# Counting GpSimd's row gathers on three semaphores in turn, in an attention and codebook-FFN kernel

## The chip, the core and the metric

The kernel runs on one core of one Trainium2 chip. The metric is the device time of one execution in microseconds (us). The profile's span, from the first to the last instruction, is a little shorter than that time.

## What is computed

The input is x, 2048 tokens by 512 features, in float32. Four small layers of width 64 run first (layer norm, a long convolution by a decaying complex exponential, a two-matrix feed-forward), then a residual and a layer norm. Behind them stands a feed-forward block whose three weight matrices are stored as rows of a codebook:

```python
CS, CB, H, I = 8, 8192, 512, 1376        # codebook: 8192 rows of 8 float32
Wg = codebook[idx_gate].reshape(I, H)    # idx_gate, idx_up: (1376, 64)
Wu = codebook[idx_up].reshape(I, H)
Wd = codebook[idx_down].reshape(H, I)    # idx_down: (512, 172)
g = einsum('bsh,ih->bsi', x, Wg)
u = einsum('bsh,ih->bsi', x, Wu)
y = einsum('bsi,hi->bsh', silu(g) * u, Wd)
x = layernorm(x + y)
```

## The kernel before

Everything stays in the core's on-chip memory, and each engine has its program written out by hand, in order. Semaphores tie the engines together; there is no scheduler. The 1376 inner rows are cut into 11 tiles (`TILES`), ten of 128 rows and the last, `FULL`, of 96.

**Gate and up** weights are made by TensorE: VectorE compares indices that SyncE has spread over the partitions (`bc`) with a column of numbers to get `one_hot` (line 839), TensorE multiplies it with the codebook into `cand` (`candidates`, line 538), VectorE picks the right row with `chosen` (line 857), and TensorE sums it up (`add_up`, line 550). Such a step of four columns is a quad; there are 352. A first part of the quads runs between the pieces of the small layers, in the slots of the loop at line 681 (`SLOTS`, 22 of them); the rest between the products of the feed-forward tiles (`hidden`, `down`, loop at line 788).

**Down** weights are made by GpSimd. For tile k it issues 64 indirect DMAs (4 blocks `q` of 16 columns `j`; 48 for the last tile), each of which gathers 128 codebook rows of 32 bytes, one per partition, into `stage_down[k % RING]`. `RING` is 3, so three tiles of down weights can stand ready. There are 688 gathers in all, and after its first few constants GpSimd does nothing else. Each gather adds 16 to its semaphore when it has landed. Two waits hold GpSimd in this loop (lines 285 to 296):

- `turned_down`: before tile k from 3 on, until TensorE has transposed tile k - 3 and so freed its buffer;
- `down_in`: at every fourth gather (`BURST`), until all gathers begun so far have landed.

TensorE's `turn_down(k, n)` (line 737) waits for its bank and for `down_in`, then transposes the four blocks of the tile (line 748) into `bank[2]`. ScalarE (`down_hi`) and VectorE (`down_lo`) copy them out as `wd`. `turn_down` stands once in each tile of the loop, after slot 4 or 3 (`TURN_DOWN`), long before `down` uses `wd`.

Of the kernel before, what the change touches and what calls it, by code (L numbers as in the profile page):

```python
# [25 lines left out]
def build(nc, a, out):  # L26
# [3 lines left out]
    CB, CS = a["L0_ffn_codebook"].shape  # L30
# [5 lines left out]
    KT = V // P  # L36
# [5 lines left out]
    JD = P // CS  # L42
# [13 lines left out]
    BCS = 4  # L56
    RING = 3
    SUB = 32
    BURST = 4
    EARLY = 8  # L60
    PER_SLOT = 2
    SLOTS = ITEMS + 6
# [28 lines left out]
    with ctx:  # L91
# [3 lines left out]
        def sem(name):  # L95
            return ctx.enter_context(nc.semaphore(name))
# [22 lines left out]
        with setup_ctx, attn_ctx:  # L119
# [3 lines left out]
            def at(name, shape, dt=F32):  # L123
                return sb(name, shape, dt, attn_ctx)
# [26 lines left out]
            turn = at("turn", [P, L, P])  # L151
# [21 lines left out]
        for c in range(NC):  # L173
# [12 lines left out]
            sq2_made var2 rs2_made normed2 spread ff_made ff_back h_made hn_made  # L186
            attn_out x_added stats_made aggregated rstd_made shift_made x1_made x1_turned x1_hi x1_lo
            bc_in0 bc_in1 bc_in2 bc_in3 one_hot_made candidates chosen_made summed picked_hi picked_lo
            down_in turned_down w_hi w_lo gate_made up_made gate_silu product act_hi_made act_lo_made
            down_made down_added out_normed stored""".split()  # L190
        s = {n: sem(n) for n in sem_names}

# [66 lines left out]
        @block.gpsimd  # L259
        def _(pool):  # L260
            pool.memset(ident[:, :], 0.0).then_inc(s["consts_made"], 1)
            pool.memset(perm[:, :], 0.0).then_inc(s["consts_made"], 1)
            pool.wait_ge(s["consts_made"], 2)
            pool.affine_select(out=ident[:, :], in_=ident[:, :], compare_op=ALU.not_equal, fill=1.0, base=0,
                               pattern=[[-1, P]], channel_multiplier=1).then_inc(s["masks_made"], 1)
            pool.affine_select(out=perm[:, :], in_=perm[:, :], compare_op=ALU.not_equal, fill=1.0, base=-D,
                               pattern=[[-1, P]], channel_multiplier=1).then_inc(s["masks_made"], 1)
            pool.wait_ge(s["masks_made"], 2)
            pool.affine_select(out=perm[:, :], in_=perm[:, :], compare_op=ALU.not_equal, fill=1.0, base=D,
                               pattern=[[-1, P]], channel_multiplier=1).then_inc(s["masks_made"], 1)  # L270
            pool.memset(adder[:, :], 0.0).then_inc(s["consts_made"], 1)
            pool.wait_ge(s["consts_made"], 3)
            block8 = adder[:, SUB - CS:SUB]
            pool.memset(block8, 1.0).then_inc(s["consts_made"], 1)
            pool.iota(iota_low[:, :], pattern=[[P, LT]], base=0, channel_multiplier=1).then_inc(s["iotas_made"], 1)
            pool.iota(iota_m[:, :], pattern=[[0, 1]], base=0, channel_multiplier=1).then_inc(s["iotas_made"], 1)
            pool.wait_ge(s["consts_made"], 4)
            pool.affine_select(out=block8, in_=block8, compare_op=ALU.is_ge, fill=0.0, base=0,
                               pattern=[[-HIGH, CS]], channel_multiplier=1).then_inc(s["masks_made"], 1)
            pool.wait_ge(s["masks_made"], 4)  # L280
            pool.affine_select(out=block8, in_=block8, compare_op=ALU.is_ge, fill=0.0, base=HIGH - 1,
                               pattern=[[HIGH, CS]], channel_multiplier=-1).then_inc(s["masks_made"], 1)
            pool.wait_ge(s["index_down_in"], 16)
            begun = 0
            for k in range(TILES):
                if k >= RING:
                    pool.wait_ge(s["turned_down"], k - RING + 1)
                for q in range(KT):
                    for j in range(JD if k < FULL else REST // CS):
                        if begun and begun % BURST == 0:  # L290
                            pool.wait_ge(s["down_in"], 16 * begun)
                        column = k * JD + j
                        pool.indirect_dma_start(stage_down[k % RING][:, q, j * CS:(j + 1) * CS], None, a["L0_ffn_codebook"],  # L293
                                                bass.IndirectOffsetOnAxis(ap=idx_down[:, q, column:column + 1], axis=0)
                                                ).then_inc(s["down_in"], 16)
                        begun += 1

        @block.scalar
# [211 lines left out]
        def _(pe):  # L510
# [226 lines left out]
            def turn_down(k, n):  # L737


                if k % 2:  # L740
                    pe.wait_ge(s["w_lo"], k)
                elif k:
                    pe.wait_ge(s["down_added"], NT * (k // 2))
                else:
                    pe.wait_ge(s["x1_lo"], NT)
                pe.wait_ge(s["down_in"], 16 * KT * (k * JD + n // CS))
                for q in range(KT):
                    done = pe.transpose(bank[2][0:n, q * P:(q + 1) * P], stage_down[k % RING][:, q, 0:n], ident[:, :])  # L748
                done.then_inc(s["turned_down"], 1)
# [38 lines left out]
            for k in range(FULL):  # L788
                shares = SHARES[k % 2]
                quads = quads_of(k)  # L790
                for slot in range(len(quads) + 1):
                    if slot < len(quads):
                        candidates(quads[slot])
                        add_up(quads[slot] - 1)
                    if 1 <= slot <= NC * shares:
                        c, share = divmod(slot - 1, shares)
                        hidden(k, P, c, share, shares)
                    if slot == TURN_DOWN[k % 2]:
                        turn_down(k, P)
                    if k % 2 and 0 <= slot - FIRST_DOWN < NT:  # L800
                        down(k, P, (0, 1), slot - FIRST_DOWN, (bank[2][:, :],))
            add_up(ALL_QUADS - 1)
            for c in range(NC + 1):
                if c < NC:
                    hidden(FULL, REST, c, 0, 1)
                if c == 0:
                    turn_down(FULL, REST)
                else:
                    for t in range((c - 1) * TPC, c * TPC):
                        down(FULL, REST, (0,), t, (bank[2][:, :], cand[0][:, :], cand[1][:, :], cand[2][:, :]))  # L810
# [374 lines left out]
```

## Time and profile before

| | us |
|---|---|
| median of three runs | 1478.64 (1478.60 to 1478.94) |
| the profiled execution | 1478.19 |
| its span | 1476.4 |
| TensorE busy in it | 1404.5 (95%) |
| VectorE busy | 1131.9 (77%) |
| GpSimd busy | 718.8 (49%) |
| ScalarE busy | 272.2 (18%) |

The rows further down come from this one profiled execution. "idle before, releaser" is the time an engine stood still before an instruction and what ended it. In a timeline row "x4" means four instructions of one kind, merged; overlapping matmuls make a merged row longer than its distance to the next. "issue" is time in which the engine waited for nothing that the profile shows. The granted TensorE clock is given as a share of full speed.

### The profile page before, as it was taken

How to read it: one execution, taken by the hardware profiler on the slowest of the kernel's cores; microseconds unless marked ns; L12 is line 12 of the kernel's file. 1: busy time of each engine (PE TensorE's matmuls, PEld its weight loads, DVE VectorE, ACT ScalarE, POOL GpSimd, SP SyncE). 2: the span in 40 equal slices, each digit the busy share in tenths (PEclk: the TensorE clock that was granted, in tenths of full speed). 3: DMA queues.
4: the chain of work that ended last, by engine and by line, in shares of the span. 5: the costliest groups of instructions: out<-in, count | busy, mean ns of one | idle time of the engine just before them, and what ended most of it. 6: DMA issues, size and time to landing. Idle time of an engine off the chain costs nothing.

```text
span 1476.4 us, 21752 instructions
## 1 busy us (share of the span) xinstructions
PE 1404.5 (95%) x7795; PEld 951.5 (64%) x7795; DVE 1131.9 (77%) x2508; ACT 272.2 (18%) x458; POOL 718.8 (49%) x703
## 2 busy tenths in 40 slices
PE   6869999977999999999999999999999999999995
PEld 4535555444666776666776666776666776678873
DVE  4998888766777768787768787778877778887656
ACT  3336666523100000000000000000000000001005
POOL 4656655552265655555555656655555555500000
PEclk9989999877999999999999999999999999999997
DMA  8222212111233323333223333223333223322103
GB/s 209 39 64 47 53 46 52 39 32 23 80 85 85 75 54 81 85 85 86 75 54 82 82 88 82 67 64 82 85 84 80 67 66 83 86 74 66 46 20 114
DMA packets 94065, 105.68 MB, mean 72 GB/s; under 512 B 43966, under 2 KB 48838, under 8 KB 93959
## 3 DMA queue, kind: packets, MB, share of 16 engines
q1 hardware_dynamic: 67908, 96.45, 22.0%
q0 software_dynamic: 22016, 2.86, 5.5%
q10 hardware_dynamic: 4034, 4.98, 1.1%
q8 instruction: 63, 1.03, 0.3%
q14 instruction: 44, 0.35, 0.1%
HBM read 99.32 MB, written 4.90 MB: 71 GB/s over the span
## 4 chain that ended last, share of the span: by engine, by line
PE 91%; DVE 4%; issue 2%; ACT 1%; SPq 1%; DMA 1%; ACTq 0%; DVEq 0%
PE bank L512 46%; PE cand L512 44%; DVE one_hot L839 1%; DMA book_in<-in_L_ffn_codebook 1%; PE bank L668 1%; DVE work L823 0%; SPq L226 0%; DVE stats L1007 0%; DVE x1t_lo L823 0%; ACT x L394 0%; ACT xt L328 0%; DVE chosen L857 0%; PE bank L748 0%; DVE x L823 0%; ACT x1t_hi L398 0%
## 5 line engine op out<-in xcount | busy, mean ns | idle before, releaser
L293 POOL DMA_INDIRECT stage_down<-in_L_ffn_codebook,idx_down x688 | 716.7, 1042 | 573.0 <-DMA stage_down<-in_L_ffn_codebook,idx_down 347.9
L512 PE MATMUL cand<-one_hot,book 128*128 128x512 f32 (+1 forms) x2816 | 729.8, 402 | 12.3 <-DVE one_hot L839 12.1
L512 PEld LDWEIGHTS cand<-one_hot,book 128*128 128x128 f32 x2816 | 532.5, 192 | 151.7 <-issue 19.2
L839 DVE TENSOR_SCALAR one_hot<-bc,low_of 128x512 fp32r<-128x512 uint16 (+1 forms) x1408 | 584.3, 477 | 0.3
L857 DVE SCALAR_TENSOR_TENSOR chosen<-bc,high_of,cand 128x512 f32<-128x512 uint16 (+1 forms) x352 | 258.5, 734 | 222.9 <-PE cand L512 221.5
L512 PE MATMUL bank<-x1t_hi,w 128*128 128x512 f32 (+1 forms) x704 | 254.2, 418 | 0.7 <-DVE w L823 0.7
L512 PEld LDWEIGHTS bank<-x1t_hi,w 128*128 128x128 f32 (+1 forms) x704 | 125.8, 185 | 51.2 <-issue 29.2
L512 PE MATMUL bank<-chosen,adder 128*32 128x128 f32 (+1 forms) x2816 | 148.6, 283 | 3.8 <-DVE chosen L857 3.8
L512 PE MATMUL bank<-x1t_lo,w 128*128 128x512 f32 (+1 forms) x352 | 147.4, 419 | 0.0
L512 PEld LDWEIGHTS bank<-chosen,adder 128*32 128x32 f32 x2816 | 55.5, 108 | 133.9 <-issue 129.4
L512 PE MATMUL bank<-wd,act_hi 128*128 128x512 f32 (+1 forms) x328 | 106.4, 406 | 0.1
L347 ACT ACTIVATE w<-bank 128x128 fp32r<-128x128 f32 (+1 forms) x88 | 24.0, 272 | 440.3 <-PE bank L512 440.3
L823 DVE TENSOR_TENSOR x<-x,bank 128x512 f32<-128x512 f32 x100 | 68.1, 681 | 28.1 <-PE bank L512 27.9
L512 PEld LDWEIGHTS bank<-x1t_lo,w 128*128 128x128 f32 (+1 forms) x352 | 65.2, 185 | 23.8 <-issue 14.3
L466 ACT ACTIVATE prod<-bank 128x512 f32<-128x512 f32 (+1 forms) x44 | 26.3, 598 | 290.4 <-PE bank L512 290.4
L470 ACT ACTIVATE act_hi<-prod 128x512 fp32r<-128x512 f32 (+1 forms) x44 | 27.9, 634 | 271.8 <-DVE prod L823 271.8
L512 PEld LDWEIGHTS bank<-wd,act_hi 128*128 128x128 f32 (+1 forms) x328 | 58.4, 188 | 18.6 <-issue 6.7
L512 PE MATMUL bank<-wd,act_lo 128*128 128x512 f32 (+1 forms) x164 | 64.4, 393 | 0.0
L512 PE MATMUL bank<-work,mean_p 128*128 128x512 f32 x72 | 35.8, 614 | 6.0 <-issue 5.6
L823 DVE TENSOR_TENSOR prod<-prod,bank 128x512 f32<-128x512 f32 (+1 forms) x44 | 29.9, 679 | 10.7 <-PE bank L512 10.6
L512 PEld LDWEIGHTS bank<-wd,act_lo 128*128 128x128 f32 (+1 forms) x164 | 30.8, 188 | 7.2
L512 PE MATMUL bank<-work,w1t 64*128 64x512 f32 x64 | 31.8, 617 | 1.3 <-DVE work L1061 1.2
(163 smaller groups left out, 713.8 us busy)
## 6 DMA issues: line engine op xcount, KB each, us to landing
bc<-index_parts SPq DMA_DIRECT2D x320, 256.0 KB
stage_down<-in_L_ffn_codebook,idx_down POOLq DMA_INDIRECT x688
bc<-index_parts_rest SPq DMA_DIRECT2D x32, 192.0 KB
x<-in_L_attn_x ACTq DMA_DIRECT2D x4, 1024.0 KB, 9.9
out_x<-x SPq DMA_DIRECT2D x16, 256.0 KB, 2.0
index_parts<-parts_t SPq DMA_DIRECT2D x20, 32.0 KB, 1.9
w_in<-in_L_attn_W ACTq DMA_DIRECT2D x2, 256.0 KB, 8.5
idx_down<-in_L_ffn_idx_down SPq DMA_DIRECT2D x1, 344.0 KB, 7.1
```

The source lines that it names most:

```text
L293: pool.indirect_dma_start(stage_down[k % RING][:, q, j * CS:(j + 1) * CS], None, a["L0_ffn_codebook"], bass.IndirectOffsetOnAxis(ap=idx_do ...
L347: act.activation(w[group % WRING][:, 0, 0:nw], bank[3 + group % 2][:, 0:nw], ACT.Copy).then_inc(s["picked_hi"], 1)
L466: act.activation(prod[0:n, c % 2, :], bank[0][0:n, :], ACT.Silu).then_inc(s["gate_silu"], 1)
L470: act.activation(act_hi[0:n, k % 2, c * C:(c + 1) * C], prod[0:n, c % 2, :], ACT.Copy).then_inc(s["act_hi_made"], 1)
L512: return pe.matmul(dst, lhs, rhs, start=start, stop=stop)
L668: done = pe.transpose(bank[2][:, k * P:(k + 1) * P], x[:, tile, k * P:(k + 1) * P], ident[:, :])
L823: return v.tensor_tensor(o, x0, x1, op)
L839: done = v.tensor_scalar(one_hot[quad % 2][:, q, 0:nw], bc[quad % BCS][:, 0:nw], low_of[:, q:q + 1], None, ALU.is_equal)
L857: v.scalar_tensor_tensor(chosen[quad % 2][:, 0:nw], bc[quad % BCS][:, nw:2 * nw], high_of[:, 0:1], cand[quad % 3][:, 0:nw], ALU.is_equal, ...
```

## The change

The single counter `down_in` becomes three, `down_in0` to `down_in2`. The gathers take them in turn: gather number `begun` adds to counter `begun % 3`. Before each gather from the fourth on, GpSimd waits until the earlier gathers of the same counter have landed, which is the gather three places ahead. The drain at every fourth gather is gone. TensorE's `turn_down` waits for all three counters, each up to the number of its gathers in the tiles so far. Buffers, gathers, their order and their tiles stay as they are.

```diff
-    BURST = 4
+    IN_FLIGHT = 3
...
                     for j in range(JD if k < FULL else REST // CS):
-                        if begun and begun % BURST == 0:
-                            pool.wait_ge(s["down_in"], 16 * begun)
+                        turn, before = begun % IN_FLIGHT, begun // IN_FLIGHT
+                        if before:
+                            pool.wait_ge(s[f"down_in{turn}"], 16 * before)
                         column = k * JD + j
                         pool.indirect_dma_start(stage_down[k % RING][:, q, j * CS:(j + 1) * CS], None, a["L0_ffn_codebook"],
                                                 bass.IndirectOffsetOnAxis(ap=idx_down[:, q, column:column + 1], axis=0)
-                                                ).then_inc(s["down_in"], 16)
+                                                ).then_inc(s[f"down_in{turn}"], 16)
                         begun += 1
...
-                pe.wait_ge(s["down_in"], 16 * KT * (k * JD + n // CS))
+                landed = KT * (k * JD + n // CS)
+                for turn in range(IN_FLIGHT):
+                    pe.wait_ge(s[f"down_in{turn}"], 16 * ((landed + IN_FLIGHT - 1 - turn) // IN_FLIGHT))
```

GpSimd's instructions, from the end of tile 2's gathers to the start of tile 3's, were these (the name in brackets is the semaphore waited for):

```order
L293 DMA stage_down2<-in_L0_ffn_codebook,idx_down 128x8 [waits down_in]
L293 DMA stage_down2<-in_L0_ffn_codebook,idx_down 128x8 x3
L293 DMA stage_down0<-in_L0_ffn_codebook,idx_down 128x8 [waits down_in,turned_down]
L293 DMA stage_down0<-in_L0_ffn_codebook,idx_down 128x8 x3
L293 DMA stage_down0<-in_L0_ffn_codebook,idx_down 128x8 [waits down_in]
```

And now:

```order
L294 DMA stage_down2<-in_L0_ffn_codebook,idx_down 128x8 [waits down_in0]
L294 DMA stage_down2<-in_L0_ffn_codebook,idx_down 128x8 [waits down_in1]
L294 DMA stage_down2<-in_L0_ffn_codebook,idx_down 128x8 [waits down_in2]
L294 DMA stage_down0<-in_L0_ffn_codebook,idx_down 128x8 [waits down_in0,turned_down]
L294 DMA stage_down0<-in_L0_ffn_codebook,idx_down 128x8 [waits down_in1]
L294 DMA stage_down0<-in_L0_ffn_codebook,idx_down 128x8 [waits down_in2]
```

No gather has moved; a wait stands before each of them, where it stood before one in four.

On TensorE, the stretch around the first `turn_down` read:

```order
L512 MATMUL bank<-x1t_hi,w 128x512 [waits x_added]
L748 MATMUL bank<-ident,stage_down 128x128 [waits down_in,x1_lo]
L748 MATMUL bank<-ident,stage_down 128x128 x3
L512 MATMUL cand<-one_hot,book 128x512 [waits chosen_made,one_hot_made]
L512 MATMUL cand<-one_hot,book 128x512 x7
```

And now:

```order
L513 MATMUL bank<-x1t_hi,w 128x512 [waits x_added]
L751 MATMUL bank<-ident,stage_down 128x128 [waits down_in1,down_in2,down_in0,x1_lo]
L751 MATMUL bank<-ident,stage_down 128x128 x3
L513 MATMUL cand<-one_hot,book 128x512 [waits chosen_made,one_hot_made]
L513 MATMUL cand<-one_hot,book 128x512 x7
```

The transposes stay in their place and carry two waits more, in each of the 11 tiles.

## Rows read from the trace of the kernel before

**Rows 1.** The page's chain that ended last, shares of the span by engine.

```profile
PE 91%; DVE 4%; issue 2%; ACT 1%; SPq 1%; DMA 1%; ACTq 0%; DVEq 0%
```

**Rows 2.** Busy time (x instructions) of PE, PEld, DVE, ACT, POOL; clock, DMA.

```profile
389.00:1292.00 903.00, 901.50 (x5330) 633.99 (x5330) 701.58 (x1485) 64.34 (x142) 517.17 (x496) 1.00 0.32 78
```

**Rows 3.** GpSimd's waits: total us, times, longest.

```profile
POOL stage_down L293 <- DMA stage_down<-in_L_ffn_codebook,idx_down: 347.9, 169, 4.7
POOL stage_down L293 <- PE bank L748: 41.2, 1, 41.2
```

**Rows 4.** GpSimd's timeline where tile 9 ends: start, us, [idle before <-releaser].

```profile
1201.03 1.16 POOL L293 DMA_INDIRECT stage_down<-in_L_ffn_codebook,idx_down  x1 [0.30 <-issue]
1204.83 1.15 POOL L293 DMA_INDIRECT stage_down<-in_L_ffn_codebook,idx_down  x1 [2.64 <-DMA stage_down<-in_L_ffn_codebook,idx_down]
```

**Rows 5.** Gathers by stretch: PE, PEld, POOL busy (x instructions) on `stage_down`; clock, DMA.

```profile
123.00:200.00 77.00, 0.00 (x0) 0.00 (x0) 46.20 (x44) 1.00 0.22 48
200.00:280.00 80.00, 0.00 (x0) 0.00 (x0) 44.40 (x42) 1.00 0.23 52
280.00:349.00 69.00, 0.00 (x0) 0.00 (x0) 40.94 (x43) 0.73 0.13 26
```

**Rows 6.** TensorE's timeline around the transposes of tile 0, and of tile 9.

```profile
389.04 0.63 PE L512 MATMUL bank<-x1t_hi,w 128*128 128x512 f32 x2
389.51 0.60 PE L748 MATMUL bank<-ident,stage_down 128*128 128x128 f32 x4
389.87 2.11 PE L512 MATMUL cand<-one_hot,book 128*128 128x512 f32 x8
...
1332.37 0.60 PE L748 MATMUL bank<-ident,stage_down 128*128 128x128 f32 x4
```

**Rows 7.** One line's instructions: duration ns min/median/max, first and last start.

```profile
L293 POOL DMA_INDIRECT stage_down<-in_L_ffn_codebook,idx_down x688: 938/947/2333, 9.1 to 1291.9; - x172
L1081 DVE TENSOR_TENSOR_SCAN work<-cols,state,work x12: 1284/1284/1335, 104.1 to 261.8; 128x512 f32<-128x512 f32 x12
```

**Rows 8.** By form, busy us, mean ns: DVE 349 to 389, DVE and POOL 1180 to 1290.

```profile
L839 DVE TENSOR_SCALAR one_hot<-bc,low_of 128x512 fp32r<-128x512 uint16 x32 | 13.3, 480 | 0.0
...
L839 DVE TENSOR_SCALAR one_hot<-bc,low_of 128x512 fp32r<-128x512 uint16 x125 | 53.2, 488 | 0.0
...
L293 POOL DMA_INDIRECT stage_down<-in_L_ffn_codebook,idx_down x59 | 61.5, 1042 | 48.8 <-DMA stage_down<-in_L_ffn_codebook,idx_down 32.0 <-issue 16.9
```

**Rows 9.** TensorE's timeline: the same matmuls at three slots of the small layers.

```profile
146.22 1.98 PE L512 MATMUL bank<-work,w2t 128*128 128x512 f32 x4
...
157.47 1.98 PE L512 MATMUL bank<-work,w2t 128*128 128x512 f32 x4
...
202.27 1.98 PE L512 MATMUL bank<-work,w2t 128*128 128x512 f32 x4
...
213.60 1.98 PE L512 MATMUL bank<-work,w2t 128*128 128x512 f32 x4
```

**Rows 10.** The chain of waits at the start: start, us, what.

```profile
14.10 0.04 issue
14.14 11.62 DMA book_in<-in_L_ffn_codebook
```

**Rows 11.** GpSimd's timeline from its first gather.

```profile
9.06 1.11 POOL L293 DMA_INDIRECT stage_down<-in_L_ffn_codebook,idx_down  x1 [5.89 <-DMA idx_down<-in_L_ffn_idx_down]
...
18.62 0.94 POOL L293 DMA_INDIRECT stage_down<-in_L_ffn_codebook,idx_down  x1 [4.71 <-DMA stage_down<-in_L_ffn_codebook,idx_down]
...
26.18 1.11 POOL L293 DMA_INDIRECT stage_down<-in_L_ffn_codebook,idx_down  x1 [2.88 <-DMA stage_down<-in_L_ffn_codebook,idx_down]
```

**Rows 12.** TensorE's timeline, three output projections of the small layers.

```profile
285.16 6.87 PE L512 MATMUL bank<-woutt,work 65*128 65x512 f32 x8 [1.20 <-ACT work L441]
...
309.22 7.10 PE L512 MATMUL bank<-woutt,work 65*128 65x512 f32 x8
...
329.54 7.10 PE L512 MATMUL bank<-woutt,work 65*128 65x512 f32 x8
```

**Rows 13.** The page's DMA queue of the gathers: packets, MB, share of 16 engines.

```profile
q0 software_dynamic: 22016, 2.86, 5.5%
```

More of the change, by code:

```diff
@@ L188, in build @@
             bc_in0 bc_in1 bc_in2 bc_in3 one_hot_made candidates chosen_made summed picked_hi picked_lo
-            down_in turned_down w_hi w_lo gate_made up_made gate_silu product act_hi_made act_lo_made
+            down_in0 down_in1 down_in2 turned_down w_hi w_lo gate_made up_made gate_silu product act_hi_made act_lo_made
             down_made down_added out_normed stored""".split()
```

## The prediction

> **What bounds the kernel now.** I read four views, in this order. First the chain that ended last: TensorE holds 91% of it, and neither GpSimd nor a gather appears in it [rows 1]. Then the busy time of the long stretch in which the feed-forward tiles run, 389 to 1292 us: TensorE is busy for 901.50 of 903.00 us at the full clock, while GpSimd issues its last 496 gathers [rows 2]. So from 389 us on the time is TensorE's own instructions. Then GpSimd's waits: it stands 347.9 us for gathers to land, 169 times, and once, for 41.2 us, for TensorE to free a buffer [rows 3]. The reader is to see that these are large numbers on an engine that nobody waits for. The last view says how far nobody waits: the last gather of tile 9 starts at 1201.03 and has landed before the next starts at 1204.83 [rows 4]; TensorE transposes that tile at 1332.37 [rows 6], 127.5 us later. I worked the same distance out for the other ten tiles and it is larger in each (134 us for the last, 153 or more for the rest). The down weights are early everywhere.
>
> **What the change does to GpSimd.** A drain costs, from the start of the fourth gather to the start of the next, 3.80 us at the end of tile 9 [rows 4]; over the whole trace half of the drains lie between 2.6 and 3.4 us. Without a wait a gather follows the one ahead after its own time plus 0.30 us: 0.95 + 0.30 = 1.25 at the least [rows 4, 7], and 1.04 + 0.30, some 1.35 to 1.40, as a mean [rows 4, 8]. A burst of four now takes about 3 x 1.38 + 2.95 = 7.1 us, or 1.77 per gather. In the changed kernel the gather three places ahead began 3 x 1.38 = 4.1 us before. Its landing is due 2.6 to 3.4 us after its start, up to 4 in a tenth of the cases, so the new wait is nearly always over when it is reached. What a finished wait costs on GpSimd no row shows; the chain's smallest piece between two instructions of a queue is 0.04 us [rows 10], and I take 1.38 + 0.05 = 1.43 us per gather. Below, it can't be under 1.25; above, if a finished wait were as dear as the 0.30 us step, 1.7.
>
> At 1.43 us, tiles 0 to 2 (192 gathers) are issued by 9.06 + 275 = 284 us instead of 349, and then GpSimd waits for TensorE's transposes of tile 0 at 389.51 [rows 6], 105 us instead of 41. From there each tile takes 64 x 1.43 = 92 us where TensorE uses a tile in about 107, so GpSimd stands at nearly every tile for `turned_down`, 10 to 30 us each time. The last gather starts near 1192 instead of 1292. The 347.9 us for landing shrink to under 40, and most of it comes back as waiting for TensorE. The change swaps one wait off the path for another off the path. The gain on the end is **0**.
>
> **What it puts on the path.** Four terms, none of them seen in the trace as such.
>
> (a) TensorE has two waits more at each of 11 transposes, 22 in all. Queued behind them is all that TensorE does, so their price would count in full. Today the first transpose carries two waits. The two matmuls ahead start at 389.04, the transposes at 389.51, 0.235 us per matmul, the same pace as without a wait [rows 6]; so two finished waits are hidden under a matmul of 512 columns. All counters are 127 us and more past their value. Lower end 0. Upper end: two more are not hidden at all and cost 0.07 each (a little over the 0.04 of [rows 10]): 22 x 0.07 = 1.5 us. I take 0, the nearest row.
>
> (b) At the start the chain runs through the load of the codebook, `book_in`, 14.14 to 25.76 [rows 10]. Gathers run beside it: two bursts, eight gathers, begin before it lands [rows 11]. A gather takes 0.055 x 1476 / 688 = 0.12 us of all 16 DMA engines [rows 13, 7]. In turn, with the slow landings of this stretch, there would be between 6 (three per 9.56 us, the time from the first gather to the end of the first drain) and 13 (one per 1.3 us). That is -2 to +5 gathers, -0.2 to +0.6 us. I take 0: the landings here are slow, which holds the rate near today's.
>
> (c) From 123 to 280 us, in the slots of the small layers, TensorE and VectorE hand work to and fro, and a delay of VectorE can reach the end. Today 44 + 42 = 86 gathers start there [rows 5]; at 1.43 us it would be 157 / 1.43 = 110, or 24 more. What does a gather do to VectorE? With GpSimd silent (349 to 389) a `one_hot` compare takes 480 ns, with 59 gathers beside it (1180 to 1290) 488 ns [rows 8]. That is 125 x 8 ns = 1.0 us for 59 gathers, 0.017 us each. Upper end 24 x 0.017 = 0.4 us. Lower end 0: two whole slots of TensorE are 157.47 - 146.22 = 11.25 us with 7 gathers started in them, and 213.60 - 202.27 = 11.33 with 5 [rows 9], so more gathers didn't make a slot longer. I take 0.
>
> (d) From 280 to 349 us all but about three of 43 gathers leave [rows 5]. By the same 0.017 us that gives back up to 0.7 us, and by the slots 0. I take 0.
>
> A rule of the Trainium skill speaks against (c). The trace shows that gathers and VectorE do meet, and who loses: a gather lasts 947 ns as a median and up to 2333, while VectorE's longest instruction of the slots, the scan, lasts 1284 and at most 1335 [rows 7]. The Trainium skill, page "SBUF — State Buffer", section "Who interferes with whom", says that the two engines share a pair of ports under an exclusive lock, that the loser is blocked for a whole instruction, and that it is issue order that decides who loses. By that rule a denser stream of gathers would win more often. The trace agrees only for the gathers' side, and the sum above stays with the rows.
>
> **The sum.** 0 + 0 + 0 + 0 + 0, against the profiled execution's 1478.19 us (span 1476.4 and 1.8 outside it). That execution lies 0.45 under the median of the runs, so I forecast on the median: **1478.6 us**. The ends of the terms give -0.2 - 0.7 = -0.9 and 1.5 + 0.6 + 0.4 = +2.5; with 0.3 for the spread of the runs the forecast's own range is 1477.4 to 1481.4.
>
> **The rivals.**
>
> *Gathers hold VectorE (slower).* Place: the slots, 123 to 280 us. Price: if each of the 24 added gathers stopped VectorE for its whole 0.94 us on the path, 22.6 us: 1501. It decides from the point at which VectorE's instructions there lengthen, or start late, by over 0.13 us per added gather (3 us over 24). For it: VectorE is busy for 64 of 73 us in these slots, with little room. Against: the scan grew by 51 ns at most [rows 7], and slots don't follow the number of gathers [rows 9]. Also, no gather is added in total before 389 us, so what is lost in the slots is in part returned by 349. Chance 0.03.
>
> *Waits on TensorE are dear (slower).* If the two added waits at each transpose cost as much as the whole 0.235 us that now hides two, each, it is 22 x 0.235 = 5.2 us: 1483.8. Against: the pace before the transposes is untouched by the two that are there [rows 6]. Chance 0.02.
>
> *The granted clock of 280 to 389 us moves (either way).* TensorE stands idle often enough there for its clock to fall: the mean was 0.73 of full over 280 to 349 [rows 5], so between its levels of 1.2 and 2.4 GHz it was at the lower half the time. From one projection to the next it took 309.22 - 285.16 = 24.06 us and then 20.32 [rows 12]. The work is nearly the same; 3.7 us is what such a stretch can win or lose by where the low clock falls. With the gathers gone from here VectorE could hand over earlier or the pattern could shift: 1474.9 (chance 0.04) or 1482.3 (0.03). Against: three executions agree within 0.34 us, so the pattern is stable.
>
> *The change does not do what it says.* If landings are slower one behind the other, or each wait costs as much as a drain's share, gathers stay at 1.77 us and GpSimd ends near 1290. The time is the same, 1478.6. Chance 0.02.
>
> **How the numbers follow.** The forecast has 0.86. It and the last rival lie within 0.2% (3.0 us, about what a measurement of this kernel can tell from no change): 0.88 same. Faster is the clock's one side, 0.04. Slower is 0.03 + 0.02 + 0.03 = 0.08. The forecast's own range leaves out all rivals but the last, 0.12 in all, and takes in the ends of every unknown cost, so it is the range given.
>
> **What would show it right or wrong.** In the profile of the changed kernel: GpSimd's waits for landing fall from 347.9 us to under 40 and its waits for TensorE rise from 41 us to some 250; gathers in a row start 1.43 us apart (1.25 to 1.7); tiles 0 to 2 are issued by about 284 us, the last gather starts near 1192. TensorE's transposes are at 389.5 and 1332.4 within 1 us, with no gap ahead of them (term a). `book_in` lands at 25.8 within 0.6 (b). The slots of the small layers stay at 11.25 us, `one_hot` at 480 ns (c). If a transpose ever waits for a gather, or if the compares or the scan grow by a tenth, my reading of what is off the path is wrong.

## The result and the profile after

| | time, us | against before on the same chip |
|---|---|---|
| before | 1478.62 (1477.45 to 1478.94) | |
| changed | 2205.18 (2190.93 to 2207.99) | 1.489 [1.486, 1.493] |

The changed kernel is 49% slower where I had forecast no change. The page of the profiled execution, 2207.99 us with a span of 2206.2, has TensorE at 67% of the span. The chain that ended last was nearly TensorE alone in [rows 1] (91%); now TensorE holds 57%, a quarter has no known releaser, and an eighth is "issue", time in which an engine waited for nothing that the profile shows:

```profile
PE 1488.9 (67%) x7795; PEld 986.0 (45%) x7795; DVE 1127.9 (51%) x2508; ACT 272.1 (12%) x458; POOL 669.3 (30%) x703
...
PE 57%; another core or an unknown queue 24%; issue 12%; DVE 5%; ACT 1%; DMA 0%; SPq 0%; DVEq 0%; ACTq 0%
...
L294 POOL DMA_INDIRECT stage_down<-in_L_ffn_codebook,idx_down x688 | 667.2, 970 | 1200.1 <-PE bank L751 974.9
```

The waits of all engines in the changed kernel (us in total, times, longest) read on from there:

```profile
POOL stage_down L294 <- PE bank L751: 974.9, 8, 332.9
DVE chosen L860 <- remote: 684.2, 31, 55.7
ACT prod L467 <- remote: 485.5, 8, 77.3
...
PE bank L513 <- DVE chosen L860: 258.3, 24, 32.4
...
PE bank L513 <- issue: 172.8, 25, 31.5
...
POOL stage_down L294 <- DMA stage_down<-in_L_ffn_codebook,idx_down: 11.4, 11, 2.9
```

GpSimd did what the change says: its waits for landings went from the 347.9 us of [rows 3] to 11.4, and gathers follow each other at 0.95 + 0.30 = 1.25 us. At the end of each stream it waits for TensorE. The news is in the others. VectorE starts `chosen` up to 55.7 us late, on data that the profile can't place ("remote", though there is one core).

Where the time goes is seen by stretches of the changed kernel: the stream of tiles 0 to 2, the pause until the first transposes, the stream of tile 3, and what follows. The columns are those of [rows 2]:

```profile
9.10:261.50 252.40, 66.14 (x283) 41.42 (x281) 49.55 (x206) 22.30 (x40) 186.54 (x192) 0.60 0.18 30
261.50:593.40 331.90, 278.27 (x1167) 153.16 (x1168) 251.78 (x509) 154.21 (x222) 0.00 (x0) 0.88 0.15 43
594.20:676.50 82.30, 30.40 (x144) 18.43 (x142) 17.15 (x37) 1.24 (x3) 62.13 (x64) 0.65 0.15 26
676.50:780.00 103.50, 82.85 (x480) 56.57 (x480) 62.12 (x134) 7.09 (x15) 23.16 (x24) 0.90 0.23 63
```

The first of these stretches in the kernel before:

```profile
9.10:261.50 252.40, 228.20 (x1018) 128.46 (x1017) 213.00 (x526) 131.34 (x186) 147.05 (x140) 0.95 0.30 67
```

While gathers run without a pause, everything else crawls: of 252 us TensorE is busy for 66, where it was busy for 228, and ScalarE for 22 in place of 131. Once they stop, the others work again. TensorE's transposes of the down weights date the delay, changed kernel first:

```profile
L751 PE MATMUL bank<-ident,stage_down x44: 270/272/274, 593.4 to 2160.7; 128*128 128x128 f32 x40, 128*96 128x128 f32 x4
```

```profile
L748 PE MATMUL bank<-ident,stage_down x44: 270/272/273, 389.5 to 1430.9; 128*128 128x128 f32 x40, 128*96 128x128 f32 x4
```

The first ones start at 593.4 in place of 389.5 us, 204 us late; the last ones are 730 us late. So 526 us came in the eight single tiles that were streamed after the first three, 66 us for each.

How an engine is held shows in the changed kernel's timeline in the stream of tile 3 (start us, us, what, [idle before <-releaser]); the matmuls shown are five of the eight of one `cand` group, which has neither wait nor signal between its matmuls:

```profile
641.03 0.59 PE L513 MATMUL cand<-one_hot,book 128*128 128x512 f32 x1 [0.74 <-issue]
641.71 0.95 POOL L294 DMA_INDIRECT stage_down<-in_L_ffn_codebook,idx_down  x1 [0.30 <-issue]
...
642.96 0.95 POOL L294 DMA_INDIRECT stage_down<-in_L_ffn_codebook,idx_down  x1 [0.30 <-issue]
643.12 0.59 PE L513 MATMUL cand<-one_hot,book 128*128 128x512 f32 x1 [1.50 <-issue]
...
648.02 0.59 PE L513 MATMUL cand<-one_hot,book 128*128 128x512 f32 x1 [2.21 <-issue]
...
650.82 0.59 PE L513 MATMUL cand<-one_hot,book 128*128 128x512 f32 x1 [2.21 <-issue]
...
653.62 0.59 PE L513 MATMUL cand<-one_hot,book 128*128 128x512 f32 x1 [2.21 <-issue]
```

Each matmul takes its 0.59 us. They start 2.09 and later 2.80 us apart, where they need no more than their own time. An instruction that waits for nothing is held too, so it is not a late semaphore alone. And the work itself did not grow: VectorE is busy for 1127.9 us in all, where it was busy for 1131.9, and ScalarE for 272.1 in place of 272.2. GpSimd's own steps stay at 0.30 us.

### The profile page after: what moved, and what is told of

It reads as the page before. It is cut to its first block, busy times and chain, and to the rows that moved or that the text cites. A ratio compares the mean times of both kernels' runs of the same rounds, so it can differ in the third digit from the quotient of the medians.

```text
span 2206.2 us, 21763 instructions
## 1 busy us (share of the span) xinstructions
PE 1488.9 (67%) x7795; PEld 986.0 (45%) x7795; DVE 1127.9 (51%) x2508; ACT 272.1 (12%) x458; POOL 669.3 (30%) x703
## 2 busy tenths in 40 slices
DMA packets 94064, 105.68 MB, mean 48 GB/s; under 512 B 43965, under 2 KB 48837, under 8 KB 93958
## 4 chain that ended last, share of the span: by engine, by line
PE 57%; another core or an unknown queue 24%; issue 12%; DVE 5%; ACT 1%; DMA 0%; SPq 0%; DVEq 0%; ACTq 0%
PE bank L513 29%; PE cand L513 28%; DVE one_hot L842 2%; DVE chosen L860 0%; DVE stats L1010 0%; PE bank L669 0%; DVE x L826 0%; DMA work<-in_L_ffn_idx_gate 0%; DVE act_lo L826 0%; DVE prod L826 0%; DVE x1t_lo L826 0%; ACT x L395 0%; PE bank L751 0%; ACT xt L329 0%
## 5 line engine op out<-in xcount | busy, mean ns | idle before, releaser
L294 POOL DMA_INDIRECT stage_down<-in_L_ffn_codebook,idx_down x688 | 667.2, 970 | 1200.1 <-PE bank L751 974.9
L513 PE MATMUL cand<-one_hot,book 128*128 128x512 f32 (+1 forms) x2816 | 777.6, 415 | 138.4 <-issue 120.3
L513 PEld LDWEIGHTS cand<-one_hot,book 128*128 128x128 f32 x2816 | 552.7, 199 | 302.3 <-issue 164.7
L513 PE MATMUL bank<-chosen,adder 128*32 128x128 f32 (+1 forms) x2816 | 154.6, 293 | 386.5 <-DVE chosen L860 258.3
L513 PE MATMUL bank<-x1t_hi,w 128*128 128x512 f32 (+1 forms) x704 | 270.0, 441 | 12.1 <-issue 11.4
L513 PEld LDWEIGHTS bank<-x1t_hi,w 128*128 128x128 f32 (+1 forms) x704 | 133.9, 197 | 67.4 <-issue 44.3
L513 PE MATMUL bank<-x1t_lo,w 128*128 128x512 f32 (+1 forms) x352 | 155.0, 440 | 7.4 <-issue 7.4
L523 PE MATMUL bank<-ident,idx_low 128*128 128x128 f32 x11 | 4.8, 441 | 107.3 <-issue 99.0
```

What stands on the lines that cost most here:

```text
L513: return pe.matmul(dst, lhs, rhs, start=start, stop=stop)
L523: done = pe.transpose(dst[0:JP, m * P:(m + 1) * P], part[:, k, :], ident[:, :])
```

## The experiments

The kernels ran in five groups ("calls" in the recorded expectations), each group on one chip, no two on the same, with the kernel before beside the others (medians 1476.98 to 1477.75 us in all groups). It turned out to matter which group a kernel ran in, so they are told in their order.

### First group: what is it in the change?

Three edits of the kernel before that keep or drop parts of the change, and the changed kernel slowed down.

`e1_three_drained`: the changed kernel's counters and TensorE's waits, with the old drain.

```diff
-                        if before:
-                            pool.wait_ge(s[f"down_in{turn}"], 16 * before)
+                        if begun and begun % 4 == 0:
+                            for other in range(IN_FLIGHT):
+                                pool.wait_ge(s[f"down_in{other}"], ...)
```

> The changed kernel with its three counters and TensorE's three waits, but GpSimd again lets everything land before every fourth gather (it waits for all three counters there) and waits at no other. Theory A, the other engines fall behind while gathers follow each other without a pause: the time is back at the kernel before, 1478 to 1480 us, gathers 1.77 us apart as a mean, and no stall marked 'remote' on VectorE. Theory B, the counters or TensorE's two extra waits do it: it stays near 2205 us. This run also gives the price of the 22 extra waits on TensorE: 0 to 1.5 us.

Measured: 1478.31 us, ratio 1.001 [1.000, 1.002]. Three counters and 22 more waits on TensorE cost nothing that can be seen: term (a) was right. Between its two theories e1 can't decide, because on this chip, as e2 and its later twin show, not even a stream without drains is held up.

`e2_one_burst64` and `e3_burst8`: the kernel before, one counter, fewer drains.

```diff
-    BURST = 4
+    BURST = 64
```

> The kernel before with its single counter, BURST 64 in place of 4: GpSimd drains only once a tile, so the gathers of a tile follow each other 1.25 to 1.35 us apart with no wait between them. Theory A (a stream without a pause holds the other engines up): near the changed kernel, 2100 to 2300 us. Theory B (three counters in turn, or a wait ahead of each gather): as before, 1478 us.

> The kernel before with BURST 8. A gather every (8 x 1.33 + 1.65) / 8 = some 1.55 us as a mean. Theory A1, what counts is that a pause comes before a backlog of 10 to 20 gathers has built up (in the changed kernel the first late hand-over came some 13 us after the stream of tile 3 began): 8 gathers last 10 us, so near 1478, up to 1500 us. Theory A2, what counts is the mean rate, with a limit between 1.77 and 1.33 us per gather: 1550 to 1900 us.

Measured: 1477.76 us, ratio 1.000 [0.999, 1.001], and 1477.5 us. In e2 gathers run 1.25 us apart at the least and 1.32 to 1.44 on average, and tiles 0 to 2 are issued by 278 us. That is what I had forecast for the change, mechanism and time, and it seemed to say that a dense stream is harmless.

`e4_paced`: the changed kernel with a GpSimd write of 128x512 ahead of each gather.

```diff
+                        pool.memset(pace[:, :], 0.0).then_inc(s["paced"], 1)
+                        pool.wait_ge(s["paced"], begun + 1)
```

> The changed kernel with a write of 128 x 512 zeros by GpSimd ahead of each gather, into a tile that nobody reads: gathers 1.8 to 2.0 us apart, three counters, a wait ahead of each, no drain. Theory A2 (mean rate): back near 1478 us, since the rate is that of the kernel before. Theory A3 (the queue has to run empty now and then, whatever the rate): 1900 to 2300 us.

Measured: 1519.92 us, 1.029 [1.027, 1.031], gathers 1.88 to 2.01 us apart, nothing "remote" (which the later groups put down to the chip at least as much as to the pace). The 43 us have another cause, and one form points to it, the `one_hot` compare between 500 and 1100 us: first the kernel before, then e4 (busy us, mean ns):

```profile
L839 DVE TENSOR_SCALAR one_hot<-bc,low_of 128x512 fp32r<-128x512 uint16 x677 | 285.6, 484 | 0.0
```

```profile
L846 DVE TENSOR_SCALAR one_hot<-bc,low_of 128x512 fp32r<-128x512 uint16 x659 | 409.7, 682 | 0.0
```

and e2, where gathers follow each other with no write between them:

```profile
L839 DVE TENSOR_SCALAR one_hot<-bc,low_of 128x512 fp32r<-128x512 uint16 x677 | 287.5, 487 | 0.0
```

GpSimd's writes of a mean 656 ns lengthen VectorE's compares by 198 ns; gathers alone don't. Here the rule that I weighed before can be placed. The Trainium skill, page "SBUF — State Buffer", section "Who interferes with whom", says that a VectorE instruction in one of its two-port modes and GpSimd lock each other out of shared ports for whole instructions. Whether the compare runs in such a mode no row shows. The trace agrees for GpSimd's writes, which lengthen the compares, and not for its gathers, which don't.

### Second and third group: counters, waits or order?

If e2 is fast and the changed kernel slow at one pace, the difference should lie in counters or waits. Eight kernels took it apart, the four f on one chip and the four g on another.

```diff
 # f1_three_burst64, f3_eight_counters, f4_two_counters (from the changed kernel)
+                        if begun and begun % 64 == 0:      # f1: in place of the wait in turn
-    IN_FLIGHT = 3
+    IN_FLIGHT = 8                                          # f3; f4: 2
 # f2_burst64_idle_waits, g2_idle_wait_every4 (e2 with a wait that is long over)
+                        if begun % 4 == 0:                 # g2 only
+                        pool.wait_ge(s["index_down_in"], 16)
 # g1_turn_every4, g4_bursts_in_turn (the counter changes at every fourth gather; g1 waits as f1
 # does, g4 ahead of each burst of four; TensorE's counts follow)
+                        turn, before = begun // 4 % IN_FLIGHT, begun // 4 // IN_FLIGHT
 # g3_small_write (f1, and ahead of each gather)
+        pace = sb("pace", [P, 8])
+                        pool.memset(pace[:, :], 0.0).then_inc(s["paced"], 1)
```

> Three counters in turn as in the changed kernel, but GpSimd waits for them only at every 64th gather, so the gathers follow each other 1.25 to 1.4 us apart with no wait ahead. Theory C, the counters taken in turn, at this pace, hold the other engines up: 1900 to 2300 us. Theory D, it takes a wait ahead of each gather: 1478 us, as with one counter and the same pace.

> One counter, a drain at every 64th gather, and ahead of each gather a wait on a semaphore that has had its value since the start (index_down_in). Pace 1.25 to 1.4 us. Theory D1, any wait ahead of each gather at this pace, even a finished one on a quiet semaphore: 1900 to 2300 us. Theory D2, only a wait on a counter that gathers in flight are adding to, or that has just been added to: 1478 us.

> The changed kernel with eight counters in place of three: each gather waits for the one eight places ahead, which landed some 7 us earlier (8 x 1.33 less 3), and TensorE's transposes wait for eight counters. Theory D2a, the wait must meet a counter that was added to within the last microsecond or two: 1478 us, plus 0 to 4 us for the 55 more waits on TensorE. Theory D1 or C: 1900 to 2300 us.

> The changed kernel with two counters: each gather waits for the one two places ahead, and this wait is really waited (a landing takes some 2.95 us from the start, two places are 2.5 to 2.7), so 1.5 to 1.6 us per gather. If the pace decides together with the waits (threshold between 1.35 and 1.96 us): 1478 to 1700 us. If waits on counters in flight decide whatever the pace: 2000 us and more.

> Three counters, but the counter is changed only after every fourth gather, and GpSimd waits for all of them at every 64th gather; pace 1.25 to 1.4 us. Theory E, a gather that changes the counter or carries a wait costs the other engines more than a plain one, and it is the sum at this pace that overruns: a quarter of the changes, near 1478, up to 1550 us. Theory F, more than one counter added to at this pace is enough: 2000 us and more.

> One counter, a drain at every 64th gather, and a finished wait on a quiet semaphore ahead of every fourth gather (of every one it gave 2236 us). Theory E: near 1478, up to 1550 us. Theory F': any waits inside a stream at this pace: 2000 us and more.

> Three counters in turn with a drain at every 64th gather (2252 us), and a write of 128 x 8 zeros by GpSimd ahead of each gather, which takes some 0.1 us and brings the pace to 1.4 to 1.6 us. If the pace decides (threshold between 1.36 and 1.74 us): between 1480 and 1900 us. If the change of counter decides whatever the pace below 1.96: over 2000 us.

> A counter per burst of four gathers, three in turn; the first gather of a burst waits for the burst three places ahead, which has long landed. No drain, one wait and one change of counter per four gathers, pace 1.25 to 1.4 us. Theory E: 1478 us or up to 1550 (one gather in four of the costly kind). Theory F: 2000 us and more. A drain-free order at the old time would show that the drain's absence is harmless.

| kernel | us | ratio to before |
|---|---|---|
| f1, three counters, drain at 64 | 2251.88 | 1.524 |
| f2, one counter, drain at 64, finished wait at each | 2235.90 | 1.513 |
| f3, eight counters in turn | 2251.14 | 1.524 |
| f4, two counters in turn | 1667.51 | 1.129 |
| g1, counter changes at each fourth, drain at 64 | 2255.64 | 1.526 |
| g2, one counter, drain at 64, finished wait at each fourth | 2232.75 | 1.511 |
| g3, f1 with a small write ahead of each gather | 1822.54 | 1.233 |
| g4, wait for the burst three places ahead | 2250.80 | 1.524 |

No count of semaphores, and no kind of wait, sets the time. It goes with the pace: those at 1.25 to 1.35 us a gather (mean over a tile) all take 2230 us or more; f4, which paces itself at 1.32 to 1.62 us over tiles 0 to 2 and at 1.72 to 1.76 later, is held up in the first part alone (its first transposes and its last are both 184 us late); g3 at 1.38 to 1.51 us is held up in part. And g2 is e2 with a finished wait at every fourth gather. That such waits should cost 755 us is no explanation, so e2 itself became the suspect. It had run in the first group, on another chip.

### Fourth group: the same kernels on another chip

> The kernel before with BURST = 64, line for line as in e2_one_burst64: one counter, gathers at most 1.3 us apart, and a wait on the last landing only at every 64th. It ran at 1477.76 us in another call than the kernels at about 2240 us that differ from it by finished waits alone. Theory A (the order of the instructions decides, and a stream of gathers with no wait between them is harmless): 1478 us again, gathers 1.32 to 1.44 us apart on average, first transposes at about 389.5 us, beside a changed kernel at 2205 us. Theory B (it is the place or moment of the call that decides, and any stream at 1.25 to 1.3 us holds the other engines up where the changed kernel is held up): 2230 to 2260 us, first transposes near 590 us, beside a changed kernel at 2205 us; and if the changed kernel runs at 1478 us here, B in its other half.

> The changed kernel, unaltered. Theory A: 2205 us as in the comparison (2190.93 to 2207.99), whatever h1 gives. Theory B: slow or fast together with h1: 2205 us beside h1 at 2230 to 2260, or about 1478 to 1481 us beside h1 at 1478.

> The kernel before with BURST = 16: a wait on the last landing at every sixteenth gather, so runs of sixteen gathers at about 1.25 us with some 3 us behind each. Theory A: 1478 us. Theory B: the pace over a tile is (16 x 1.25 + 3) / 16 = 1.44 us a gather, at which the kernel with three counters and a small write ahead of each gather took 1822.54 us; if only the mean pace counts, 1700 to 1900 us; if a backlog is worked off in each 3 us gap, 1478 us.

> The kernel before with BURST = 8 as in e3_burst8 (1477.5 us there). Mean pace (8 x 1.25 + 3) / 8 = 1.63 us a gather. Theory A: 1477 to 1479 us. Theory B: also 1477 to 1479 us if the limit lies between 1.5 and 1.6 us a gather, as the runs with two counters say (held up at 1.32 to 1.36 us, not at 1.72 to 1.76); above 1500 us if this run too owed its time to its call.

The edits are `BURST = 64`, none to the changed kernel, `BURST = 16`, `BURST = 8`. Measured: h1 2235.19 us, ratio 1.512 [1.506, 1.518], where its twin e2 had 1477.76; h2 2210.77, 1.493 [1.487, 1.500]; h3 2119.41, a median of four from 2076.95 to 2131.76, too spread for an interval; h4 1499.88, 1.014 [1.010, 1.019], where its twin e3 had 1477.5. Theory B of these texts holds: the chip or the moment decides, and e2 was no proof that a dense stream is harmless. The kernel before, beside them, took 1477.29 us, so a drain at every fourth gather is what sets it apart from h1. It also places the limit on such a chip. Runs of 4 gathers cost nothing, runs of 8 cost 23 us (1.4%, small but clear of the spread), runs of 16 cost 642 and of 64 758. The forecast for h3 by the mean pace alone, 1700 to 1900 us, was too low: a run of 16 with 3 us behind it is not worked off.

### Fifth group: instructions or rows?

`i1_half_rows` fetches 64 rows with each gather and so leaves out half of the down codes; e2's code runs once more beside it (`i2_one_burst64_beside`).

```diff
+                pool.memset(stage_down[b][HALF:P, :, :], 0.0).then_inc(s["half_cleared"], 1)
-                        pool.indirect_dma_start(stage_down[k % RING][:, q, j * CS:(j + 1) * CS], None, ...,
-                                                bass.IndirectOffsetOnAxis(ap=idx_down[:, q, column:column + 1], axis=0)
+                        pool.indirect_dma_start(stage_down[k % RING][0:HALF, q, j * CS:(j + 1) * CS], None, ...,
+                                                bass.IndirectOffsetOnAxis(ap=idx_down[0:HALF, q, column:column + 1], axis=0)
```

> The kernel before with BURST = 64 and each gather fetching 64 rows in place of 128; the lower 64 partitions of the three stages are cleared once at the start and the rest of the down codes are left out, so the output misses them. As many gather instructions and as many signals as in i2, half the rows and half the bytes. Theory A (what the other engines are held up by goes with the gather instructions or with their signals): slow like i2, 2200 us or more, the more so if a gather of 64 rows takes GpSimd less than 0.95 us and the gathers come closer together than 1.25 us. Theory B (it goes with the rows, each a transfer of 32 bytes of its own): below 1520 us, if the limit is 1.5 us for 128 rows and the gathers of 64 rows stay over 0.75 us apart. Between the two, 1520 to 2200 us: both count.

> The kernel before with BURST = 64 once more, on the same chip as i1: 2230 to 2260 us where the chip is of the kind on which four calls showed the hold-up, and 1478 us where it is of the kind of the call in which e2 ran; in that case i1 tells nothing.

Measured: 1477.2 us (10 runs), 0.999 [0.998, 1.000], and 1478.19 us (10 runs), 1.001 [0.999, 1.002]. The group had landed on a chip without the hold-up, so i1 tells nothing of its cause. What it does tell is the price of a gather: with half the rows an instruction has a mean of 1026 ns in place of 1057, so GpSimd's time for it hardly goes with its rows.

But i2 and h1 are one program in two groups, and that is the cleanest pair of all. Their windows, i2 first (columns as above):

```profile
60.00:90.00 30.00, 15.99 (x79) 9.78 (x78) 28.58 (x97) 3.92 (x9) 23.29 (x23) 0.79 0.28 60
230.00:260.00 30.00, 30.00 (x129) 16.17 (x128) 27.17 (x52) 18.07 (x25) 23.60 (x22) 1.00 0.27 56
```

```profile
60.00:90.00 30.00, 13.32 (x36) 7.95 (x36) 2.25 (x17) 2.08 (x3) 22.00 (x24) 0.61 0.07 4
230.00:260.00 30.00, 10.01 (x36) 5.46 (x36) 0.00 (x0) 2.77 (x4) 19.11 (x21) 0.61 0.05 3
```

GpSimd starts as many gathers in both, 23 and 24 in the first window. VectorE does 28.58 us of work in one and 2.25 in the other. Over the whole program the mean pace differs too, 1.32 to 1.44 us a gather over a tile in i2 and 1.25 to 1.36 in h1. That is in part a result of the hold-up: a gather lasts 1057 ns as a mean in i2, and 966 in h1, where VectorE stands still beside it. So the pace of a held kernel is not wholly a cause. The granted clock of 0.61, nearer TensorE's 1.2 than its 2.4 GHz, comes with the idling and is not its cause: VectorE and ScalarE stand still as well.

h4, with runs of 8, lies between. It is held up mostly at the start: its first transposes are 16 us late and its last 23.

```profile
L748 PE MATMUL bank<-ident,stage_down x44: 270/272/274, 405.5 to 1453.8; 128*128 128x128 f32 x40, 128*96 128x128 f32 x4
```

By 230 us its engines are as busy as i2's:

```profile
60.00:90.00 30.00, 21.43 (x110) 13.85 (x106) 23.88 (x97) 6.68 (x16) 21.27 (x21) 0.83 0.18 34
230.00:260.00 30.00, 30.00 (x132) 15.46 (x131) 27.00 (x48) 19.22 (x26) 20.92 (x19) 1.00 0.23 47
```

### What the missing records say

"Remote" means that the event which released an instruction is not in the trace. I counted the semaphore updates that the traces hold in the 140 us from 100 to 240 us after the first of them, inside the stream of tiles 0 to 2, and over the whole execution:

| kernel | group | time, us | updates in 140 us | in all |
|---|---|---|---|---|
| before | comparison | 1478.62 | 2008 | 20661 |
| e2 and i2, drain at 64 | first and fifth | 1477.76, 1478.19 | 2294, 2250 | 20495, 20562 |
| h4, drain at 8 | fourth | 1499.88 | 1154 | 11154 |
| h1, drain at 64 | fourth | 2235.19 | 199 | 10246 |
| changed | comparison | 2205.18 | 201 | 10310 |

Each gather raises its counter by 16, in single updates: 688 x 16 = 11008 are due, and before has 10968 of them recorded, h1 1533. In the stream h1 keeps 1.4 updates a microsecond, where its gathers alone, at 1.25 us, raise 12.8. From 30 to 120 us of the span it is flat, 13 to 16 updates in each 10 us, where e2 has between 141 and 343. h4 has lost nearly half of its records (its twin e3 has 2117 and 20578) and hardly any time, so records can go missing where engines are hardly held. Only these records are missing: h1 and i2 have 21752 instructions and 94064 DMA packets each.

That points at the path on which the chip writes its event records: it may be full, and then stop those who write to it. This would explain that all engines are held and that an instruction without a wait is held too, and would leave room for chips that differ. The Trainium skill, page "NOTIFIC — the notification-queue block", section "Overflow: three behaviours, one of which stalls the engine", says that in one of its modes a record is dropped where its queue is full, and that the block's internal pipeline always holds back rather than lose a record. By that rule, with the engines as producers, the program would show no hold-up where nothing is recorded. No run here shows that part: every execution, the timed ones too, has a recorded span and clock. So the cause is argued from the counts and not shown.

## Why the prediction was wrong, point by point

- **What bounds the kernel, and that nobody waits for a gather**: right, and still so. TensorE's transposes waited for no gather in the changed kernel, e2, i2 or h4. "The gain on the end is 0" held as far as gain goes: e2 and i2 drop nearly all landing waits and run at 1478 us.
- **GpSimd's side**: landing waits 11.4 us (under 40 forecast), but 974.9 us of waiting for TensorE and not some 250, since TensorE itself was late. A step of 1.25 us, not 1.43: a finished wait on GpSimd costs nothing, and the gather's mean fell to 970 ns, as beside a VectorE that stands still. Tiles 0 to 2 were issued by 261 us, not 284. The denser stream is the dangerous end of my own bracket, 1.25 to 1.7 us, and I asked only whether it would change when gathers are done.
- **The step that failed is "The change swaps one wait off the path for another off the path", with term (c) as its price.** I priced a gather's effect on others at 0.017 us from stretches at today's pace, with a drain after every fourth [rows 5, 8, 9], and multiplied by the 24 added ones. The effect isn't in proportion. At four in a run it is nil, and at 1.25 us without a break the stretch to the first transposes costs 204 us, and each later tile 66. The drain that looked idle in [rows 4] was what kept the others running. I read the drain as a wait that does nothing, and never asked for what it spares.
- **(a)** 0, confirmed by e1 on a chip without the hold-up. **(b)** `book` is cast from 25.3 us on, so `book_in` had landed within 0.6 of 25.8: confirmed. **(d)** is lost under the rest: in 280 to 349 us the changed kernel is catching up.
- **The rivals.** "Gathers hold VectorE" came closest, with a chance of 0.03 and 22.6 us. Its test, VectorE starting late by over 0.13 us per added gather, was met many times over. Its mechanism and price were wrong: VectorE's instructions did not lengthen, and TensorE and ScalarE are held as well. Its "Against", that no scan grew and that slots don't follow the number of gathers, came from rows with a drain every four gathers, which can't speak of a stream without one. The rule of the Trainium skill that I set against (c) pointed to the same side for another reason. I had left out that the page ties it to certain forms of VectorE's instructions; e4 fits that reason for writes only. That the gathers' own length (947 to 2333 ns) shows who loses was argued from one trace; i2 and h1 bear it out (1057 and 966 ns). Dear waits on TensorE are ruled out by e1, and the fall of the granted clock, to a mean of 0.81, followed the idling.
- **The signs of being wrong** that I named were a transpose waiting for a gather and compares or scans longer by a tenth. Neither came: all 44 transposes start without a wait, `one_hot` has a mean of 477 ns in both kernels, and the scans stay at 1284 ns. They could catch only a hold-up by longer instructions.
- **The range** had no end for a resource that the trace of before never loads. For a change that makes an engine issue without a pause, the nearest rows were no bound.
- On the chips of the first and fifth group the forecast would probably have held, by e2 and i2. The changed kernel itself did not run there.

No kernel here beats the one before. Its medians are 1477 to 1479 us in the comparison and in all five groups; a longer burst wins nothing where it is harmless, and loses elsewhere.

## What to carry to other kernels

A pause on an engine that nobody waits for can still be a throttle: before taking it out, ask what rate the engine will run at then, how much of that the trace has ever shown, and forecast a tail for it. Keep a small bound on GpSimd's gathers in a row; here a drain at every fourth was free, at every eighth cost up to 23 us, and at every 64th up to 758. When two near-equal programs that ran on different chips differ wildly, run both files side by side on one chip before reading anything into the edit.

## What the runs showed of the hardware

- A row gather takes GpSimd 0.95 us and 0.30 to the next, for 128 rows and nearly the same for 64 (means of 1057 and 1026 ns, and 966 for 128 rows beside idle engines); a finished wait between two adds nothing.
- An unbroken stream of these, 1.25 us apart at the least, held TensorE, VectorE and ScalarE on three chips and in the comparison (2191 to 2257 us), and not on two others (1474 to 1483 us); one and the same program, e2, i2 and h1, is among both. Where it was held, the limit lay between runs of 4 and 16 gathers, with a small cost at 8, and between the 1.38 to 1.51 us a gather of g3, held in part, and the 1.72 to 1.76 of f4's later tiles, not held.
- With it most semaphore updates of the stream are missing from the trace (199 in 140 us, where gathers alone raise some 1790), so that waits are put down to "remote". In a program of one core such a label was here a sign of missing records.
- Beside GpSimd writes of 128x512 VectorE's 128x512 compares took 682 ns in place of 484; gathers left them at 487.

Open are whether the chip or the moment decides (no chip was used for two groups), and what differs there; whether the program is held up when nothing is recorded; and whether the gathers' instructions, signals or rows load the full resource; i1, which was to tell, ran on a chip without the effect.
